# First group of a four-group adapter/FFN kernel: table product behind the fourth mixing step, and the first weight tile made alone among the steps

## The chip, the cores and the metric

One Trainium2 chip, one core of it. The metric is device time in microseconds (us) of one execution, median over runs. TensorE is called PE here, VectorE DVE, ScalarE ACT, GpSimd POOL and SyncE SP; each takes its instructions in the order in which they are written, and they meet only through semaphores.

## The reference, cut to what matters

`x` is 32 x 64 x 1024 in float32, that is 2048 tokens of 1024 columns.

```python
def _L0_cond_ref(x, weights, condition):
    return jnp.einsum('bct,bcd->bdt', x, weights[condition])   # 64 x 64 mix of the rows of a batch
def _L0_ffn_ref(x, W_base, b_base, enc0, enc1, coefs0, coefs1, mask0, mask1):
    base = jnp.einsum('bsd,od->bso', x, W_base) + b_base
    e0, e1 = (jnp.einsum('bsd,rd->bsr', x, e) for e in (enc0, enc1))
    w0, w1 = coefs0 * mask0, coefs1 * mask1
    decoded = jnp.einsum('bsr,eor->ebso', e0, w0) + jnp.einsum('bsr,eor->ebso', e1, w1)
    return base + real_fourier_orthogonal_multiply(decoded).sum(axis=0) * 0.5
# then x = x + L0 ; x = x + sign-weight layer(LoRA gate/up/down MLP(x))
```

The Fourier step is linear. So the first layer is one 1024 x 1024 product with an **effective weight**: W_base plus (encoder rows)^T times a low-rank matrix of 40 rows, and that matrix is the masked, summed coefficients times a fixed 1024 x 1024 Fourier table.

## The kernel before, in words

The tokens go through in four groups of 512 (`g` = 0 to 3). A float32 product is made of three passes over words of a shorter type: high x high, high x low, low x high. ACT writes the high word (`copy`), DVE the low word, the difference (`lo`, L862). Three PE lines, L1404 to L1406, are those three passes.

Each group begins with eight **mixing steps** (`mixing`, `e` = 0 to 7; two for each 128 tokens), which mix the tokens and turn them at once. ACT copies each step's result out twice, DVE makes its low word. Then comes the **first layer**, eight products `first_layer(u)`, each with one weight tile of 128 output columns; `u` = 0 and 1 are cut in two halves of 256 tokens, of which half 0 needs only the first four mixing steps.

In the first group the effective weight must be made first. Its parts:

- SP loads, in this order: x tiles 0 to 2, coefficients and masks, x tile 3, encoder rows, the table (2 MB in four loads), W_base tiles 0 to 3, the bias columns, W_base tiles 4 to 7. There are four slots for W_base tiles: the load of tile u from 4 on waits until tile u-4 is turned (`base_turned`, `load_base`, L277).
- `adapter_sum` (DVE) makes the sums of the coefficients; `low_rank_product` (PE, L1648) multiplies them by the table, into PSUM banks 6 and 7.
- `low_rank_rows` (DVE, L1286 to L1290, then `stacked`, L1265 and L1269) forms the low-rank matrix as the sum and the difference of the two banks, with its words. 120 stacked rows hold the three passes, so a weight tile is one pass.
- `turn_base(u)` (DVE, L1252) transposes a W_base tile, `weight_pair(v)` (PE, L1637) makes the low-rank part of two tiles in banks 2 to 5, `add_weight(u)` (DVE, L1260) adds it, `made_unit(u)` (ACT, then DVE) splits the tile into words, `store_weight(u)` (a DMA on ACT's queue) puts it to memory for the groups to come.

PE's order in the first group: steps 0 to 5, table product, steps 6 and 7, pair 0, first layer 0 and 1 with pair 1 between, pair 2, first layer 2 and 3, pair 3, first layer 4 to 7, then the ranks of the next layer (L1477). DVE's order behind the steps is `effective_weight` and then `first_layer_all`: for each u the total of tile u (`x1_total`, L1033), for some u an `add_weight`, a transpose of a later weight ("beside"), `made_unit(3 + u)`, the low word of the total and the low words of the beside weight. The semaphore `w_added` counts added tiles.

POOL issues the loads of the adapters: A factors first (16 loads), then B factors (16), then 32 small ones.

Of the kernel before, what the change touches and what calls it, by code (L numbers as in the profile page):

```python
# [29 lines left out]
P = 128  # L30
H = 1024
# [68 lines left out]
WEIGHT_BANKS = 2  # L100
# [15 lines left out]
def build_layers(nc, x, cond_index, lora_index, cond_w, W_base, b_base, enc0, enc1, coefs, masks, fourier, scratch,  # L116
# [6 lines left out]
    with ExitStack() as ctx:  # L123
# [83 lines left out]
        kept_step, wsum_done, g_psum, g_read = sem("kept_step"), sem("wsum_done"), sem("g_psum"), sem("g_read")  # L207
# [55 lines left out]
        def _(sp):  # L263
# [147 lines left out]
            for i in range(2):  # L411
                sp.dma_start(coef[i], coefs[i].rearrange("e (p c) r -> p e (c r)", c=KC)).then_inc(coef_in, 16)
                sp.dma_start(coef_mask[i], masks[i].rearrange("e (p c) r -> p e (c r)", c=KC)).then_inc(coef_in, 16)
            load_x(0, 3)
# [3 lines left out]
            table_rows = fourier.rearrange("(p c) n -> p c n", c=KC)  # L418
            for i in range(4):
                sp.dma_start(table[:, 2 * i:2 * i + 2], table_rows[:, 2 * i:2 * i + 2]).then_inc(table_in[i], 16)  # L420
# [28 lines left out]
        def _(pool):  # L449
# [63 lines left out]
            def group(g):  # L513
                index = chosen(lora_index, g)
                wait(piece_lo, START + LOW_PIECES * g)
# [3 lines left out]
                load_b(index, 0)  # L519
# [61 lines left out]
        def _(act):  # L581
# [182 lines left out]

            def mixing_all(g, weights):
# [15 lines left out]
            def first_layer_all(g, making):  # L781

                act.wait_ge(out_psum, START + 8 * g)
                for u in range(KC):
# [6 lines left out]
                    if making and u in (0, 1, 3, 4):  # L791
                        store_weight(u + 4 - u // 3)
# [54 lines left out]
            mixing_ahead(0)  # L847
            mixing_all(0, False)
            for u in range(3):
                made_unit(u)  # L850
                store_weight(u)
            store_weight(3)
# [6 lines left out]
        def _(dve):  # L859
# [359 lines left out]
            def mixing_all(g, weights, beside=None):  # L1219
                for e in range(8):  # L1220
                    if beside is not None:
                        beside(e)
# [32 lines left out]
            def add_weight(u):  # L1255
                dve.wait_ge(base_turned, u + 1)
                dve.wait_ge(w_psum, u // 2 + 1)
                tile = base_t[:, u].rearrange("p (k o) -> p k o", k=KC)
                made = ps[:, WEIGHT_BANKS:WEIGHT_BANKS + 4, :].rearrange("p a (k n o) -> p (a k) n o", k=2, n=2)
                dve.tensor_tensor(tile, made[:, :, u % 2, :], tile, ALU.add).then_inc(w_added, 1)  # L1260

            def stacked(dst, src, column, done):

                low = own_sb[0:STACK, GB + column:GB + column + 1]
                dve.tensor_copy(dst, src).then_inc(g_read, 1)  # L1265
                dve.wait_ge(g_read, done)
                parts = [(dst[:, q], src[:, q]) for q in range(4)] if len(dst.shape) == 4 else [(dst, src)]
                for to, full in parts:
                    last = dve.scalar_tensor_tensor(out=to, in0=to.bitcast(F32), scalar=low, in1=full, op0=ALU.mult,  # L1269
                                                    op1=ALU.add)  # L1270
                last.then_inc(g_read, 1)

            def low_rank_rows(e):

                if e == 1:
                    adapter_sum()
                if e == 3:
                    dve.wait_ge(enc_in, 96)
                    stacked(enc_s.rearrange("r k (q d) -> r q k d", q=4),
                            enc.rearrange("r (q k d) -> r q k d", q=4, k=KC), 0, 1)  # L1280
                if e != 6:
                    return
                turn_base(0)
                near, far = low_rank[:, 0:H // 2], low_rank[:, H // 2:H]
                dve.wait_ge(g_psum, 1)
# [8 lines left out]
            def effective_weight():  # L1294
# [12 lines left out]
                for u in range(5, KC):  # L1307
                    turn_base(u)
# [459 lines left out]
```

## Time and profile before

| | us |
|---|---|
| median of 3 runs | 1940.35 (1940.18 to 1941.18) |
| the profiled execution | 1939.93 |
| its span, first to last instruction | 1938.2 |
| PE busy in the span | 1912.8 (99%) |
| DVE busy | 1493.0 (77%) |
| ACT busy | 763.3 (39%) |
| DMA, mean rate | 113 GB/s |

The profiled execution lies 0.42 us under the median; 1.7 us of it lie outside the span. The page has the busy shares of the engines, a picture of the span in 40 slices, the DMA queues, the chain of work that ended last and the costliest groups of instructions. The first of the 40 slices (the first 48 us) is the only one but for the last with PE below nine tenths. For a stretch this short the order of time is read: the timeline of an engine, with the idle time before an instruction and who ended it.

### The profile page before, as it was taken

The page shows a single profiled execution, that of the slowest core. Times are in us where ns is not written, and L with a number is a line of the kernel's source. Part 1 is how long each engine was busy: PE and PEld are TensorE (multiplying, and loading weights), DVE is VectorE, ACT ScalarE, POOL GpSimd, SP SyncE. Part 2 cuts the span into 40 slices and gives each one's busy share as a digit, 9 for nine tenths or more (in the row PEclk, how much of TensorE's full clock was granted, in tenths as well). Part 3 has the DMA queues.
Part 4 walks back from the last instruction along what each step waited for, and adds up shares of the span by engine and source line. Part 5 has one row for each costly group of instructions (what it writes and reads, how often), then busy time and mean ns, then how long its engine had stood idle before and what let it go on. Part 6 is the DMA issues. An engine that isn't in the chain of part 4 may idle for free.

```text
span 1938.2 us, 31467 instructions
## 1 busy us (share of the span) xinstructions
PE 1912.8 (99%) x9088; PEld 1605.7 (83%) x9088; DVE 1493.0 (77%) x2484; ACT 763.3 (39%) x1450; POOL 543.9 (28%) x935
## 2 busy tenths in 40 slices
PE   6999999999999999999999999999999999999998
PEld 5888888888988888888898888888889888888887
DVE  6977777778778777777777877777877787777786
ACT  3453333334344343333344434333335443334331
POOL 6442222213415212211523322212071322222100
PEclk9999999999999999999999999999999999999999
DMA  9675445543476554444447655454334655555411
GB/s 245 152 147 108 103 98 116 121 94 82 126 149 127 106 115 100 101 99 88 119 116 143 124 113 110 106 116 99 70 102 131 139 121 110 121 110 113 99 44 44
DMA packets 320629, 219.43 MB, mean 113 GB/s; under 512 B 177192, under 2 KB 311208, under 8 KB 320544
## 3 DMA queue, kind: packets, MB, share of 16 engines
q1 hardware_dynamic: 281952, 189.47, 43.5%
q0 software_dynamic: 36352, 24.19, 7.0%
q10 hardware_dynamic: 2240, 4.72, 0.7%
q8 instruction: 42, 0.69, 0.2%
q14 instruction: 43, 0.35, 0.1%
HBM read 205.40 MB, written 12.58 MB: 112 GB/s over the span
## 4 chain that ended last, share of the span: by engine, by line
PE 92%; DVE 4%; issue 2%; ACT 2%; DMA 0%; POOLq 0%; DVEq 0%; ACTq 0%; POOL 0%
PE ps L1404 26%; PE ps L1406 26%; PE ps L1405 26%; PE ps L1611 6%; PE ps L1538 2%; PE ps L1458 2%; PE ps L1459 2%; DVE ps L876 2%; PE ps L1430 1%; PE ps L1477 1%; PE ps L1428 1%; DVE split L862 1%; ACT split L608 0%; ACT hidden L608 0%; PE ps L1648 0%
## 5 line engine op out<-in xcount | busy, mean ns | idle before, releaser
L1404 PE MATMUL ps<-x,split 128*128 128x512 f32 x1376 | 537.7, 391 | 1.3 <-DVE split L862 1.3
L1406 PE MATMUL ps<-x,split 128*128 128x512 f32 x1376 | 536.3, 390 | 0.0
L1405 PE MATMUL ps<-x,split 128*128 128x512 f32 x1376 | 535.4, 389 | 0.0
L608 ACT ACTIVATE split<-ps 128x512 fp32r<-128x512 f32 x344 | 203.0, 599 | 450.8 <-DVE ps L876 438.8
L505 POOL DMA_DIRECT2D nat_ad<-L_cond_A_down x224 | 137.3, 620 | 733.4 <-DVE ps L876 724.3
L1406 PEld LDWEIGHTS ps<-x,split 128*128 128x128 f32 x1376 | 258.3, 188 | 55.8
L1405 PEld LDWEIGHTS ps<-x,split 128*128 128x128 f32 x1376 | 258.4, 188 | 54.8
L1404 PEld LDWEIGHTS ps<-x,split 128*128 128x128 f32 x1376 | 259.0, 188 | 50.0 <-DVE split L862 2.5
L1404 PE MATMUL ps<-hidden 128*128 128x512 f32 x672 | 261.5, 389 | 0.0
L1405 PE MATMUL ps<-hidden 128*128 128x512 f32 x672 | 261.5, 389 | 0.0
L1406 PE MATMUL ps<-hidden 128*128 128x512 f32 x672 | 261.4, 389 | 0.0
L862 DVE TENSOR_TENSOR split<-ps,split 128x512 fp32r<-128x512 f32 (+1 forms) x376 | 243.4, 685 | 19.3 <-ACT split L608 6.7
L876 DVE STREAM_TRANSPOSE ps<-nat 128x512 f32<-128x512 f32 x344 | 225.5, 701 | 0.5
L1118 DVE TENSOR_TENSOR acc<-ps,acc 128x512 f32<-128x512 f32 x200 | 135.2, 689 | 47.4 <-PE ps L1406 47.4
L499 POOL DMA_DIRECT2D nat_b<-L_cond_B_gate x224 | 124.5, 556 | 161.1 <-DVE ps L876 149.1
L608 ACT ACTIVATE hidden<-ps 128x512 fp32r<-128x512 f32 x184 | 109.2, 599 | 143.3 <-DVE ps L876 136.9
L1404 PEld LDWEIGHTS ps<-hidden 128*128 128x128 f32 x672 | 126.2, 188 | 26.1
L1406 PEld LDWEIGHTS ps<-hidden 128*128 128x128 f32 x672 | 126.2, 188 | 26.1
L1405 PEld LDWEIGHTS ps<-hidden 128*128 128x128 f32 x672 | 126.2, 188 | 25.9
L876 DVE STREAM_TRANSPOSE ps<-nat_down 128x512 f32<-128x512 f32 x176 | 141.0, 846 | 0.0
L1102 DVE TENSOR_TENSOR act_f<-ps,gated 128x512 f32<-128x512 f32 x84 | 58.0, 690 | 97.3 <-PE ps L1459 96.8
L583 ACT ACTIVATE hidden<-act_f 128x512 fp32r<-128x512 f32 (+1 forms) x88 | 55.6, 632 | 188.9 <-DVE act_f L1102 179.9
(137 smaller groups left out, 2830.5 us busy)
## 6 DMA issues: line engine op xcount, KB each, us to landing
nat<-L_cond_W_gate SPq DMA_DIRECT2D x336, 128.0 KB
nat<-L_cond_W_up SPq DMA_DIRECT2D x336, 128.0 KB
nat_down<-L_cond_W_down SPq DMA_DIRECT2D x112, 384.0 KB, 6.4
nat_a<-L_ffn_weight SPq DMA_DIRECT2D x128, 128.0 KB, 2.8
nat<-effective_weight SPq DMA_DIRECT2D x24, 512.0 KB
nat<-x SPq DMA_DIRECT2D x16, 512.0 KB
nat_b<-L_cond_B_gate POOLq DMA_DIRECT2D x224, 24.0 KB, 2.2
nat_b<-L_cond_B_up POOLq DMA_DIRECT2D x224, 24.0 KB, 2.1
```

The costliest lines, as they stand in the source:

```text
L499: pool.dma_start(nat_b[32 * (b // 2):32 * (b // 2) + 32, t, :, b % 2, :], b_rows[t][bass.ds(part, 1), bass.ds(i, 1)].rearrange("q a f b c ...
L505: pool.dma_start(nat_ad[b % 2::2, b // 2, :], ad_rows[bass.ds(part, 1), bass.ds(i, 1)].rearrange("q a f r c -> (q a f) r c"))\
L583: return act.activation(dst, src, ACT.Copy)
L608: act.activation(dst, src, func).then_inc(piece_hi, 1)
L862: return dve.tensor_tensor(dst, full, hi.bitcast(F32), ALU.subtract)
L876: dve.transpose(dst, src).then_inc(piece_turned, 1)
L1102: dve.tensor_tensor(act_f[:], ps[:, (2 * j + 1) % 3, :], gated[:], ALU.mult).then_inc(up_read, 1)
L1118: dve.tensor_tensor(acc[:, i, :], ps[:, DOWN_BANKS[i], :], acc[:, i, :], ALU.add).then_inc(down_added, 1)
L1404: pe.matmul(dst, a[0], b[0], start=first, stop=False)
L1405: pe.matmul(dst, a[0], b[1], start=False, stop=False)
L1406: return pe.matmul(dst, a[1], b[0], start=False, stop=last)
L1611: mm = pe.matmul(ps[:, OUT_BANKS[o], :], signs[:, m, P * o:P * o + P], down(s, m), start=(m == 0 and s == 0), stop=(m == KC - 1 and s == 1))
```

## The change

All of it is in the first group (`g` = 0).

- **SP**: the four table loads are issued ahead of x tile 3 and the encoder rows.
- **POOL**: the B factors are loaded first; the A factors wait until the table product is done.
- **PE**: the table product stands behind step 3 instead of step 5. The eight weight tiles are made in five products instead of four: tile 0 alone, behind step 5, in banks 6 and 7; tiles 1 and 2 between the halves of first layer 0; 3 and 4 between the halves of first layer 1; 5 and 6 ahead of first layer 3; 7 ahead of first layer 5. Each but the first two waits until all tiles of the one before it are added.
- **DVE and ACT**: the banks of the table product are copied out by both engines. The words of the low-rank matrix are made for tiles 0 to 2 first and for the others later. Tiles 0 and 1 are added, split and awaited by halves of their rows. The first copy of the encoder rows moves from DVE to ACT. The orders of both engines are written out (`mixing_first`). DVE now adds tiles 3 to 7 in first-layer steps u = 0 to 4 (before: tiles 4 to 7 in steps 0, 1, 3, 4).

```diff
+MADE = ((0,), (1, 2), (3, 4), (5, 6), (7,))
+MADE_BANKS = (6, 2, 2, 2, 4)
+LOW_COLUMNS = (slice(0, 96), slice(96, 256))
...
+            for i in range(4):
+                sp.dma_start(table[:, 2 * i:2 * i + 2], table_rows[:, 2 * i:2 * i + 2]).then_inc(table_in[i], 16)
             load_x(0, 3)
...
-            for i in range(4):
-                sp.dma_start(table[:, 2 * i:2 * i + 2], table_rows[:, 2 * i:2 * i + 2]).then_inc(table_in[i], 16)
             for u in range(BASE_SLOTS):
                 load_base(u)
...
+                if g == 0:
+                    load_b(index, 0)
+                    wait(g_psum, 1)
                 wait(piece_lo, START + LOW_PIECES * g)
                 load_a(index, A_gate, 0)
                 wait(piece_turned, PIECES * g)
                 load_a(index, A_up, 1)
-                load_b(index, 0)
+                if g > 0:
+                    load_b(index, 0)
...
+            def made_halves(u):
+                slot_read(0, 0, SPLIT_W + u)
+                hi = split[:, (SPLIT_W + u) % SPLIT_SLOTS, 0, :]
+                act.wait_ge(half_added, u + 1)
+                copy(hi[:, 0:512], base_t[:, u, 0:512]).then_inc(half_hi, 1)
+                act.wait_ge(w_added, u + 1)
+                copy(hi[:, 512:], base_t[:, u, 512:]).then_inc(plain_hi, 1)
...
@@ ScalarE, mixing_first @@
+                mixing(0, 2)
+                act.wait_ge(enc_in, 96)
+                copy(enc_s.rearrange("r k (q d) -> r q k d", q=4),
+                     enc.rearrange("r (q k d) -> r q k d", q=4, k=KC)).then_inc(enc_step, 1)
+                mixing(0, 3)
+                cond(0, 3)
+                act.wait_ge(enc_step, 2)
+                act.wait_ge(g_psum, 1)
+                copy(enc[:, 0:512], ps[0:STACK, 6, :]).then_inc(g_moved, 1)
+                for e in range(4, 6):
+                    mixing(0, e)
+                made_halves(0)
+                for e in range(6, 8):
+                    mixing(0, e)
+                store_weight(0)
+                made_halves(1)
+                store_weight(1)
+                made_unit(2)
+                store_weight(2)
...
@@ VectorE @@
+            def low_rank_words(i):
+                cols = LOW_COLUMNS[i]
+                even, odd = (enc[:, 512 * h:512 * h + 512].rearrange("r (q c) -> r q c", q=2)[:, :, cols] for h in range(2))
+                whole, words = (t.rearrange("r (q c) -> r q c", q=4) for t in (low_rank, low_s))
+                dve.wait_ge(g_moved, 2)
+                dve.tensor_tensor(whole[:, 0:2, cols], even, odd, ALU.add)
+                dve.tensor_tensor(whole[:, 2:4, cols], even, odd, ALU.subtract).then_inc(low_step, 1)
+                dve.wait_ge(low_step, 3 * i + 1)
+                dve.tensor_copy(words[:, :, cols], whole[:, :, cols]).then_inc(low_step, 1)
+                dve.wait_ge(low_step, 3 * i + 2)
+                dve.scalar_tensor_tensor(out=words[:, :, cols], in0=words[:, :, cols].bitcast(F32),
+                                         scalar=own_sb[0:STACK, GB + 1:GB + 2], in1=whole[:, :, cols], op0=ALU.mult,
+                                         op1=ALU.add).then_inc(low_step, 1)
...
@@ VectorE, mixing_first @@
+                mixing(0, 3)
+                cond(0, 3)
                 turn_base(0)
+                low_rank_out()
+                low_rank_words(0)
+                for e in range(4, 6):
+                    mixing(0, e)
+                add_weight(0)
+                made_low_half(0, 0)
+                mixing(0, 6)
+                made_low_half(0, 1)
+                mixing(0, 7)
                 turn_base(1)
+                low_rank_words(1)
+                add_weight(1)
                 turn_base(2)
+                for half in range(2):
+                    made_low_half(1, half)
+                add_weight(2)
                 turn_base(3)
                 made_unit(2)
+                for u in range(4, KC):
                     turn_base(u)
...
                     x1_total(g, u)
-                    if making and u in (0, 1, 3, 4):
-                        add_weight(u + 4 - u // 3)
+                    if making and u < 5:
+                        add_weight(3 + u)
...
@@ TensorE @@
+                    if by_halves and half == 0 and k == 0:
+                        pe.wait_ge(half_lo, u + 1)
+                    if by_halves and half == 0 and k == 4:
+                        pe.wait_ge(plain_lo, 4 + u + 1)
...
+            def make_weights(v):
+                tiles = MADE[v]
                 if v == 0:
+                    pe.wait_ge(low_step, 3)
+                elif v == 1:
                     pe.wait_ge(mixed_lo, 8)
                     pe.wait_ge(xt_copied, 8)
                 else:
+                    pe.wait_ge(low_step, 6)
+                    pe.wait_ge(w_added, MADE[v - 1][-1] + 1)
...
                 if making:
                     first_layer(g, 0, 0)
+                    make_weights(1)
                 first_layer(g, 0, 1)
                 for u in range(1, KC):
-                    if making and u in (1, 2, 4):
-                        weight_pair((u + 2) // 2)
+                    if making and u in (3, 5):
+                        make_weights((u + 3) // 2)
                     if u == 1:
                         if making:
                             first_layer(g, 1, 0)
+                            make_weights(2)
                         first_layer(g, 1, 1)
```

## Rows read from the trace of the kernel before

**Rows 1.** The page: busy us of each engine, share of the span, instructions.
```profile
PE 1912.8 (99%) x9088; PEld 1605.7 (83%) x9088; DVE 1493.0 (77%) x2484; ACT 763.3 (39%) x1450; POOL 543.9 (28%) x935
```

**Rows 2.** Stretches: length; busy PE, PEld, DVE, ACT, POOL; granted clock; DMA share, GB/s.
```profile
30.00:40.00 10.00, 4.81 (x34) 3.97 (x32) 8.75 (x10) 3.21 (x5) 7.70 (x14) 0.88 1.16 170
...
80.00:90.00 10.00, 10.00 (x46) 8.25 (x45) 10.00 (x16) 5.47 (x10) 5.39 (x7) 1.00 0.87 177
```

**Rows 3.** Timeline of PE: start, length, instruction; in brackets idle before, releaser.
```profile
20.59 0.36 PE L1428 MATMUL ps<-mix,split 128*128 128x256 f32 x1 [0.32 <-DVE mix L862]
...
23.78 7.03 PE L1648 MATMUL ps<-fourier_table,wsum 128*120 128x512 f32 x16
...
36.34 1.20 PE L1637 MATMUL ps<-low_s,enc_s 120*128 120x256 f32 x8 [2.73 <-DVE turned L862]
...
41.34 0.58 PE L1404 MATMUL ps<-turned,split 128*128 128x256 f32 x1 [3.80 <-DVE split L862]
...
56.22 0.39 PE L1404 MATMUL ps<-turned,split 128*128 128x512 f32 x1
...
61.70 0.39 PE L1404 MATMUL ps<-turned,split 128*128 128x512 f32 x1
...
67.14 1.12 PE L1637 MATMUL ps<-low_s,enc_s 120*128 120x256 f32 x8
...
68.39 0.47 PE L1404 MATMUL ps<-turned,split 128*128 128x512 f32 x1
...
90.44 4.00 PE L1477 MATMUL ps<-x,hidden 128*128 128x256 f32 x32
```

**Rows 4.** Stretches around PE's two long waits, columns as in rows 2.
```profile
37.50:38.00 0.50, 0.03 (x1) 0.00 (x0) 0.35 (x1) 0.00 (x0) 0.50 (x2) 0.63 1.03 106
...
41.30:44.40 3.10, 3.06 (x14) 3.07 (x15) 3.07 (x3) 1.06 (x1) 2.99 (x6) 0.50 1.05 321
44.40:48.50 4.10, 4.10 (x36) 4.10 (x35) 0.42 (x1) 0.00 (x0) 3.71 (x8) 0.99 1.13 297
```

**Rows 5.** Timeline of DVE.
```profile
25.25 1.28 DVE L862 TENSOR_TENSOR turned<-ps,turned 128x512 fp32r<-128x512 f32 x2
...
30.85 0.69 DVE L1286 COPY low_rank<-ps 120x512 f32<-120x512 f32 x1 [3.17 <-PE ps L1648]
...
33.75 1.28 DVE L1269 SCALAR_TENSOR_TENSOR low_s<-low_s,own_sb,low_rank 120x1024 fp32r<-120x1024 f32 x1
...
49.78 1.22 DVE L1260 TENSOR_TENSOR base_t<-ps,base_t 128x1024 f32<-128x1024 f32 x1 [4.96 <-PE ps L1637]
...
54.47 3.49 DVE L1252 STREAM_TRANSPOSE base_t<-base 128x1024 f32<-128x1024 f32 x3
57.88 0.71 DVE L1033 SCALAR_TENSOR_TENSOR acc<-ps,b_col,acc 128x512 f32<-128x512 f32 x1
...
63.33 1.22 DVE L1260 TENSOR_TENSOR base_t<-ps,base_t 128x1024 f32<-128x1024 f32 x1
```

**Rows 6.** Timeline of ACT.
```profile
60.19 1.56 ACT L583 ACTIVATE lora_b<-ps 64x256 fp32r<-64x256 f32 x4 [0.93 <-DVE ps L876]
...
73.39 1.06 ACT L583 ACTIVATE split<-base_t 128x1024 fp32r<-128x1024 f32 x1 [2.90 <-DVE base_t L1260]
```

**Rows 7.** Issues on SP's queue in three stretches, each with its times to landing.
```profile
L420 SPq DMA_DIRECT2D fourier_table<-fourier x4: 352/432/432, 10.6 to 11.9; - x4
...
DMA to landing us min/median/max: 6.4/7.7/10.2
...
L277 SPq DMA_DIRECT2D base<-L_ffn_W_base x3: 431/433/451, 36.6 to 37.5; - x3
DMA to landing us min/median/max: 3.7/3.9/3.9
...
L277 SPq DMA_DIRECT2D base<-L_ffn_W_base x4: 437/471/1050, 43.6 to 45.7; - x4
DMA to landing us min/median/max: 6.0/6.4/7.2
```

More of the change, by code:

```diff
@@ L846, in _ @@
             act.activation(gated[:, 0:1], lora_b_rem[:, 0, 0, 0:1].bitcast(F32), ACT.Silu)
[L847 to L852, printed above, removed]
+            mixing_first()
             first_layer_all(0, True)
@@ L1217, in made_unit, with made_low_half, mixing_all @@
                 lo(split[:, s, 1, :], base_t[:, u], split[:, s, 0, :]).then_inc(plain_lo, 1)
-            def mixing_all(g, weights, beside=None):
+            def made_low_half(u, half):
+                s = (SPLIT_W + u) % SPLIT_SLOTS
+                cols = slice(512 * half, 512 * half + 512)
+                if half == 0:
+                    dve.wait_ge(half_hi, u + 1)
+                else:
+                    dve.wait_ge(plain_hi, 4 + u + 1)
+                lo(split[:, s, 1, cols], base_t[:, u, cols], split[:, s, 0, cols]).then_inc((half_lo, plain_lo)[half], 1)
+            def mixing_all(g, weights):
                 for e in range(8):
-                    if beside is not None:
-                        beside(e)
                     mixing(g, e)
@@ L1255, in add_weight @@
             def add_weight(u):
+                v, n = MADE_OF[u]
                 dve.wait_ge(base_turned, u + 1)
-                dve.wait_ge(w_psum, u // 2 + 1)
+                dve.wait_ge(w_psum, v + 1)
                 tile = base_t[:, u].rearrange("p (k o) -> p k o", k=KC)
[L1259 to L1271, printed above, removed]
@@ L1294, in effective_weight @@
-            def effective_weight():
+                tiles = len(MADE[v])
+                made = ps[:, MADE_BANKS[v]:MADE_BANKS[v] + 2 * tiles, :]\
+                    .rearrange("p a (k n o) -> p (a k) n o", k=4 // tiles, n=tiles)[:, :, n, :]
+                if u < 2:
+                    dve.tensor_tensor(tile[:, 0:4], made[:, 0:4], tile[:, 0:4], ALU.add).then_inc(half_added, 1)
+                    dve.tensor_tensor(tile[:, 4:], made[:, 4:], tile[:, 4:], ALU.add).then_inc(w_added, 1)
+                else:
+                    dve.tensor_tensor(tile, made, tile, ALU.add).then_inc(w_added, 1)
@@ new lines, in enc_words @@
+            def enc_words():
+                low = own_sb[0:STACK, GB:GB + 1]
+                dst = enc_s.rearrange("r k (q d) -> r q k d", q=4)
+                src = enc.rearrange("r (q k d) -> r q k d", q=4, k=KC)
+                dve.wait_ge(enc_step, 1)
+                for q in range(4):
+                    last = dve.scalar_tensor_tensor(out=dst[:, q], in0=dst[:, q].bitcast(F32), scalar=low, in1=src[:, q],
+                                                    op0=ALU.mult, op1=ALU.add)
+                last.then_inc(enc_step, 1)
@@ L1307, in effective_weight @@
-                for u in range(5, KC):
+                for u in range(4, KC):
                     turn_base(u)
@@ L1435, in first_layer @@
                 m = SPLIT_W + u
-                pe.wait_ge(plain_lo, 12 * g + 4 + u + 1)
+                by_halves = g == 0 and u < 2
+                if not by_halves:
+                    pe.wait_ge(plain_lo, 12 * g + 4 + u + 1)
                 if half == 0:
```

76 lines of the change are left out of this document (35 added, 41 removed).

## The prediction

> **What bounds the kernel now.** I read the shares first: PE is busy 99% of the span, no other engine over 77% [rows 1]. So a change of the first group can only win back PE's idle time, and the stretches say where that is: in 30 to 40 us PE is busy for 4.81 us, and in 80 to 90 us it is full again, but so is DVE [rows 2]. PE's timeline names the waits: 2.73 us ahead of pair 0 and 3.80 us ahead of first layer 0, both ended by DVE [rows 3]. The granted clock then stands at 0.50 (1.2 GHz) from 37.6 us until PE has worked again from 41.34 to 44.4 us [rows 4]; those 3.1 us of work cost about 1.5 us. Together some 8 us, 0.4% of the time, can be won.
>
> The second thing to see is DVE. It waits 4.96 us for pair 1 and from 49.78 us on has one instruction behind the other [rows 5]. At 57.88 it takes the total of tile 0, without a wait for PE, so PE is ahead of it there. PE goes without a break from 41.34 to the ranks at 90.44 [rows 3], but with a full DVE beside it. Whatever makes PE earlier than DVE's list must be paid back as a wait.
>
> **The change, part by part.** All times below are on the clock of the profiled execution (1939.93 us, span 1938.2), which is 0.42 us under the median of the runs; the sum is made against it and then moved by 0.42.
>
> *Table product.* Steps 4 and 5 begin at 20.59 and the product at 23.78 [rows 3]; put ahead of them it begins near 20.1, as soon as step 3 is through, and ends 7.03 us later, at 27.1 instead of 30.8. It needs the table, which landed between 17.0 and 22.1 when issued at 10.6 to 11.9 [rows 7]. Issued ahead of x tile 3, whose issue waits, it lands some 5 us sooner, in time. x tile 3 and the encoder rows come behind its 2 MB. Only ACT's copies hang on them; ACT takes them in order, so a late tile delays the copies of steps 2 and 3, which nothing needs before PE takes up step 4 at 27. Cost nothing; cover 4 us and more.
>
> *POOL.* The B factors come sooner, the A factors some 10 us later, behind the wait for the table product; behind that wait stand the 32 small loads and nothing else that is urgent: the A factors are turned in first-layer step 3, 40 us later. Cost nothing on this list.
>
> *DVE's chain from 27.1 us.* A 1024-wide DVE instruction takes 1.22 us alone and 1.15 in a row (3.49 for three), a 512-wide one 0.69 and 0.60 (1.28 for two) [rows 5]. Copy out 0.7; words for tiles 0 to 2 (two adds of 192 columns, a cast and a scaled add of 384, by width from these rows and 1.28 for 1024) 1.7: 29.5. Low words of steps 4 and 5, each behind two ACT copies of 0.6: 31.6. Tile 0 by halves 1.3, its ACT half copy 0.7, low half 0.6: 34.2, where first layer 0 can start. Step 6's low word waits about 1 us for ACT, whose half copies stand ahead of it; with the second half and step 7: 36.5. Turn tile 1, other words (2.2), add tile 1, turn 2, two low halves, add 2, turn 3: 45.7. Some 15 handovers between engines add 0.4: 46.1. Low word of tile 2, turns 4 to 7: 51.9, if the tiles are there.
>
> *W_base tiles 4 to 7.* This is a wait that before hardly shows. SP issues tile 7 only when tile 3 is turned, now at 46.1, in four loads 0.44 us apart, so the last at 47.5. Times to landing: 3.7 to 3.9 us where little was queued, 6.0 to 7.2 us behind three other tiles [rows 7]. So tile 7 lands between 51.2 and 54.7; with only tile 6 ahead of it I take the near end, 51.4. DVE then begins tile 7 at 51.4 instead of 50.8 and the total of tile 0 at 52.5, against 57.88 before.
>
> The Trainium skill says (DMA: Bandwidth & Descriptors, Issuing engines are not separate DMA queues) that loads issued by SP, ACT and POOL run on the same 16 engines and interleave. It speaks against POOL's part: the A factors now travel beside W_base tiles 5 and 6, which by that rule would move the landing towards the far end. No row separates the two; the range holds both ends.
>
> *First-layer steps 0 and 1 on DVE.* Before, from the total of tile 0 to the end of the add in step 1 took 63.33 + 1.22 - 57.88 = 6.67 us [rows 5]. Now the tile split in a step is the one added in it, so DVE waits for ACT's 1.06 us copy, which starts behind the add [rows 6], with only a short transpose between: 0.9 us a step, and 0.3 us more behind the 1.56 us of ACT copies [rows 6]. Step 0 has these waits in full: 7.85 us. So the fifth tile (tile 4) is added at 52.5 + 7.85 = 60.4.
>
> *PE.* First layer 0 starts at 34.2 instead of 41.34. It waits 0.7 us for its second half, then 1.5 us for tile 1, and reaches the end of first layer 2 at about 56, where before that was 61.70 [rows 3]. There the third product of two tiles (5 and 6) waits for five added tiles: until 60.4, a **new wait of 4.4 us**. Before, the same kind of wait stood one first layer later and cost nothing. Then: this product 0.96 us, five first layers of 5.5 us (56.22 to 61.70 is 5.48; 68.39 to 90.44 is four of 5.51), tile 7's product 0.6 (half of 0.96; up to 0.96 if its cost is by instruction): 29.1. The ranks begin at 89.5, against 90.44: **0.9 us won**.
>
> *The clock.* The wait before lasted 4.0 us, with 1.2 us of pair 0 inside, when the clock fell [rows 3, 4]. A wait of 4.4 us without work is more idle than that, so I take the fall, and the cost that the same fall had before: 1.5 us, now on PE's path, since from there PE has no slack. Bounds: 0 (no fall) to 2.5 us. The Trainium skill has it so (TensorE: Matmul & The Clock Gate, What's actually happening): the lower level is the default to which an idle TensorE falls back. By that rule the sum is 0.6 us slower, without it 0.9 us faster.
>
> Sum: -0.9 + 1.5 = +0.6 us, 1940.5 in the profiled execution, **1941.0** as a median. The five first layers, and all 1840 us behind the ranks, stay as they are.
>
> **The rivals.** *A: the wait at tiles 5 and 6 doesn't come.* Then PE keeps its lead of 5.7 us: 1934.6. For it: PE's idle before is as large. Against it: DVE's instructions from 27.1 to the fifth add sum up to 29 us even with no wait among them, so 56.1 at the earliest, and its waits for ACT and loads are real. A gain over 0.2% needs the fifth add by 57.4. Chance 0.08.
>
> *B: the W_base tiles come late.* If tile 7 lands 7.2 us after its last issue or worse (54.7), the fifth add is at 63.8, PE's wait is 7.7 us, and the time is 4.0 us longer: 1944.4, growing one for one. It decides from a landing at 54.6 on. For it: stores of the finished weight tiles (512 KB each) and POOL's loads fall into the same stretch. Against it: SP's queue ahead of tile 7 is shorter than before. Chance 0.14.
>
> *C: the clock stays.* The wait is cut by an early tile 7 or the fall comes too late to matter: 1939.4. Chance 0.2.
>
> *D: the table product isn't earlier.* If the table lands late after all, at 22.1 as before, the chain begins 2 us later: 1943. The issue time speaks against it. Chance 0.03.
>
> My forecast has 0.55.
>
> **How the numbers follow.** A measurement of this kernel tells 0.2% (3.9 us) from no change. Faster by more: A, and a little of C: 0.09. Slower by more: B: 0.14. Within: 0.77. For the range, low: no wait for tile 7, DVE's chain 0.6 us shorter, no fall, 2.5 us faster, rounded down to 1937.5. High: B with little over its bound, 1944.5. A and the tail of B are left out.
>
> **What would show it.** Right: in the trace of after the table product starts near 20.1; the first product of the first layer near 34; DVE's total of tile 0 between 51.5 and 55; PE idle 3 to 8 us ahead of the product for tiles 5 and 6, ended by an add of DVE, with the clock at 0.50 behind it; from there no wait to the ranks. Wrong: a wait there under 2 us (A), a DVE wait of over 3 us ahead of the last turned tile (B), the clock at 1.00 through the wait (C), or any change of duration behind 95 us.

## The result, and the profile after

The changed kernel takes 1943.53 us (median; 1942.18 to 1944.5), the kernel before, on the same chips, 1940.29 (1939.25 to 1941.58). The ratio is 1.0015, with a 95% interval from 1.0009 to 1.0021: 3.2 us or 0.17% slower, under the 0.2% that the prediction took as the bound, though the interval ends just above it. The predicted median was 1941.0, with a range of 1937.5 to 1944.5; the time lies in the range, near its upper end. Of all executions below one, with the products later, took 4995 us; it is left out.

| | before | after |
|---|---|---|
| the profiled execution | 1939.93 | 1943.57 |
| its span | 1938.2 | 1941.9 |
| PE busy | 1912.8 | 1913.9 |
| the table product starts | 23.78 | 20.48 |
| first layer 0 starts | 41.34 | 34.45 |
| the ranks start | 90.44 | 94.13 |

The last row says where to look: the ranks come 3.69 us later, the whole span is 3.7 us longer, so nothing behind them has changed. The page's line of busy times stands for [rows 1]:

```profile
PE 1913.9 (99%) x9096; PEld 1606.2 (83%) x9096; DVE 1493.8 (77%) x2491; ACT 764.7 (39%) x1454; POOL 543.1 (28%) x935
```

Next the stretches of [rows 2], with the same columns (length; busy PE, PEld, DVE, ACT, POOL; granted clock; DMA share, GB/s):

```profile
30.00:40.00 10.00, 9.34 (x77) 8.97 (x76) 8.21 (x14) 4.33 (x9) 7.77 (x14) 1.00 1.10 202
80.00:90.00 10.00, 10.00 (x46) 8.28 (x45) 9.47 (x15) 4.65 (x8) 5.28 (x6) 1.00 0.84 193
```

From 30 to 40 us PE is now busy for 9.34 us instead of 4.81. That gap is closed. PE's timeline (start, length, instruction; in brackets the idle time before and who ended it) shows what came of it, in the places of [rows 3]:

```profile
20.48 7.13 PE L1733 MATMUL ps<-fourier_table,wsum 128*120 128x512 f32 x16
...
30.24 1.05 PE L1722 MATMUL ps<-low_s,enc_s 120*128 120x128 f32 x8
...
34.45 0.36 PE L1476 MATMUL ps<-turned,split 128*128 128x256 f32 x1 [0.31 <-DVE split L904]
...
43.45 0.35 PE L1476 MATMUL ps<-turned,split 128*128 128x256 f32 x1 [1.45 <-DVE split L904]
...
62.54 2.04 PE L1722 MATMUL ps<-low_s,enc_s 120*128 120x256 f32 x8 [6.68 <-DVE base_t L1316]
64.38 0.63 PE L1476 MATMUL ps<-turned,split 128*128 128x512 f32 x1
...
76.89 1.01 PE L1722 MATMUL ps<-low_s,enc_s 120*128 120x128 f32 x8
77.73 0.44 PE L1476 MATMUL ps<-turned,split 128*128 128x512 f32 x1
...
94.13 0.40 PE L1555 MATMUL ps<-x,hidden 128*128 128x256 f32 x2
```

The waits of 2.73 and 3.80 us are gone, and first layer 0 starts 6.9 us earlier. At the end of first layer 2 it is still 5.8 us ahead (55.86 instead of 61.70). All of that and more is given back in one place: PE stands 6.68 us ahead of the product of tiles 5 and 6, until DVE (L1316) has added the low-rank part of the fifth tile. DVE's timeline, in the places of [rows 5], says why that add ends only at 62.39 (a "turn" is DVE's transpose of a W_base tile):

```profile
44.96 1.23 DVE L1301 STREAM_TRANSPOSE base_t<-base 128x1024 f32<-128x1024 f32 x1
46.23 1.23 DVE L904 TENSOR_TENSOR split<-base_t,split 128x1024 fp32r<-128x1024 f32 x1
47.37 3.49 DVE L1301 STREAM_TRANSPOSE base_t<-base 128x1024 f32<-128x1024 f32 x3
53.45 1.25 DVE L1301 STREAM_TRANSPOSE base_t<-base 128x1024 f32<-128x1024 f32 x1 [2.59 <-DMA base<-L_ffn_W_base]
54.62 0.71 DVE L1075 SCALAR_TENSOR_TENSOR acc<-ps,b_col,acc 128x512 f32<-128x512 f32 x1
...
61.18 1.21 DVE L1316 TENSOR_TENSOR base_t<-ps,base_t 128x1024 f32<-128x1024 f32 x1
```

The first row is the turn of tile 3; its end, 46.19, frees the slot for W_base tile 7. The fourth is the turn of tile 7, which waits 2.59 us for that load. So the total of tile 0 (L1075) is at 54.62 and the fifth add 7.77 us later. The loads of tile 7 themselves, as in [rows 7] (SP's issues, then the times to landing, that is, until the data are there):

```profile
L285 SPq DMA_DIRECT2D base<-L_ffn_W_base x4: 312/696/1572, 46.2 to 49.1; - x4
...
  DVE base_t L1301: 2.6, 1
...
DMA to landing us min/median/max: 4.3/4.9/5.1
```

Last the stretches around the wait, as in [rows 4]:

```profile
50.00:55.80 5.80, 5.80 (x28) 4.55 (x26) 3.21 (x4) 0.00 (x0) 4.40 (x9) 1.00 0.38 66
55.90:62.50 6.60, 0.00 (x0) 0.00 (x0) 5.59 (x9) 2.99 (x7) 5.01 (x9) 0.88 0.29 86
62.50:67.70 5.20, 5.16 (x16) 4.51 (x17) 4.07 (x7) 3.08 (x6) 0.00 (x0) 0.50 0.26 102
67.70:76.00 8.30, 8.30 (x38) 6.78 (x38) 7.18 (x11) 4.50 (x8) 0.00 (x0) 1.00 0.43 153
```

After 55.9 us PE does nothing; the mean clock of 0.88 there means that it fell near the end of the wait. The work from 62.54 on runs at 0.50 (1.2 GHz) until 67.7: 0.63 us for a product that takes 0.39 at 1.00.

### The profile page after: what moved, and what is told of

It is laid out like the page before. It is cut to its first block, busy times and chain, and to the rows that moved or that the text cites. A ratio compares the mean times of both kernels' runs of the same rounds, so it can differ in the third digit from the quotient of the medians.

```text
span 1941.9 us, 31500 instructions
## 1 busy us (share of the span) xinstructions
PE 1913.9 (99%) x9096; PEld 1606.2 (83%) x9096; DVE 1493.8 (77%) x2491; ACT 764.7 (39%) x1454; POOL 543.1 (28%) x935
## 4 chain that ended last, share of the span: by engine, by line
PE 91%; DVE 4%; ACT 2%; issue 2%; DMA 1%; POOLq 0%; SPq 0%; DVEq 0%; ACTq 0%; POOL 0%
PE ps L1476 25%; PE ps L1478 25%; PE ps L1477 25%; PE ps L1689 6%; PE ps L1616 2%; PE ps L1536 2%; PE ps L1537 2%; DVE ps L918 2%; PE ps L1502 1%; PE ps L1555 1%; PE ps L1500 1%; DVE split L904 1%; ACT split L620 0%; ACT hidden L620 0%; PE ps L1733 0%
## 5 line engine op out<-in xcount | busy, mean ns | idle before, releaser
L1478 PEld LDWEIGHTS ps<-x,split 128*128 128x128 f32 x1376 | 258.3, 188 | 55.9
```

Of the source, the lines that this page charges most:

```text
L1478: return pe.matmul(dst, a[1], b[0], start=False, stop=last)
```

## The experiments

The runs set one theory against its rivals. Theory 1 is that of the prediction: PE's lead ends at the product of tiles 5 and 6, which waits for DVE's list; the list is held up by W_base tile 7, and the clock falls in the wait. The rivals: the other moves of the change (the table ahead of x tile 3, POOL's order) cost something by themselves, or the first group is bound elsewhere, so that taking this wait away moves it and wins nothing. Each expectation below names its own rival, as theory 2 or by a letter.

Time medians are compared with the kernel before as it ran beside them. Single executions of these kernels begin the table product anywhere from 19.9 to 21.7 us, with no edit that would explain it. So, where traces are compared, the time from the start of the table product to the ranks is used as well: 73.65 us in the profile of after, 70.9 in the prediction.

### The clock alone: the wait filled with unused products

```diff
+                    if making and u == 3:
+                        for k in range(27):
+                            pe.matmul(ps[:, 1, :], split[:, (SPLIT_W + 2) % SPLIT_SLOTS, 0, 0:P], mixed[:, 0, 0],
+                                      start=True, stop=True)
```

> Against the changed kernel, 27 products whose result is not used (some 6.1 us of work, into a bank that first layer 3 overwrites) stand in PE's wait ahead of the product of tiles 5 and 6; nothing else is changed, and DVE's list is untouched. Theory 1 (2.5 us of the loss are the lower clock that the wait brings): the clock stays at 1.00, the product of tiles 5 and 6 starts within 0.3 us of 62.5, the ranks 2.2 to 2.5 us sooner: 1941.1 us. Rival (the clock costs nothing, DVE is the bound behind it): 1943.5 us.

Measured: 1940.80 us, before 1940.96, ratio 1.0001 (0.9992 to 1.001). PE's timeline and one stretch of this kernel:

```profile
56.44 6.28 PE L1745 MATMUL ps<-turned,split 128*128 128x512 f32 x27
62.83 1.20 PE L1722 MATMUL ps<-low_s,enc_s 120*128 120x256 f32 x8
...
92.25 0.52 PE L1555 MATMUL ps<-x,hidden 128*128 128x256 f32 x3
```

```profile
40.00:92.00 52.00, 50.44 (x265) 42.95 (x264) 46.53 (x63) 20.15 (x35) 24.36 (x39) 1.00 0.64 160
```

The product of tiles 5 and 6 starts no earlier (62.83 against 62.54), but the clock stays at 1.00, and from the end of the fifth add (62.69) to the ranks it takes 29.56 us instead of 31.74. So the fall of the clock costs **2.2 us** of the changed kernel, on PE's path, as the prediction had it, and without it the change is worth nothing either way. By the changed kernel's own rows it is nearer 2.5: the product of tiles 5 and 6 takes 1.84 us to the next instruction instead of 0.96, and the eight products behind it start 0.43 us apart instead of 0.23. In the run with the wait filled, both weight products take 0.08 us more and that of tile 7 starts 0.16 us late, so its 29.56 is not quite free of waits. The medians of the two kernels lie further apart, 3.4 us against their kernels before; 0.5 us of that is a fifth add that came earlier in this trace (41.39 us behind the start of the table product instead of 41.91), and the rest is within the intervals.

That difference can be read in each run in which the same work follows the same add. The second column is what of the stretch at 0.50 lies in work, the third the time from the fifth add to the ranks, less 29.56:

| | PE's wait | work at 0.50 | price |
|---|---|---|---|
| after | 6.68 | 5.2 | 2.2 |
| small loads behind tile 7 | 4.86 | 5.4 | 2.2 |
| store of tile 2 later | 5.80 | 3.4 | 1.3 |
| both | 4.42 | 5.8 | 2.4 |
| POOL's order as before | 5.98 | 4.4 | 1.8 |
| table behind, as before | 6.42 | 3.6 | 1.4 |
| turn of tile 7 later | 3.10 | 3.4 | 1.3 |

The price is about 0.4 us for each us of work at 0.50 (up to 0.5, if 29.56 is 0.3 too long), and it does not go with the length of the wait: the longest of these waits costs less than the second shortest.

### The load of W_base tile 7: what stands beside it

Three edits, one on POOL's queue, one on ACT's, and both at once:

```diff
+                if g == 0:
+                    wait(base_turned, KC)
                 load_rest(index)
```

> The changed kernel with POOL's 32 small loads behind the transpose of W_base tile 7. Theory A (the small loads slow SP's issue and the landing of tile 7): its four loads are issued within 1.8 us of the transpose of tile 3, the last lands 5.3 us or less after that transpose ends (changed kernel: 2.9 us and 7.2 us), and DVE's wait for tile 7 is under 1 us. Theories B (the store of tile 2) and C (the way from the transpose to the landing is as long with nothing beside it): 7 us, a wait of 2.4 to 2.7 us.

```diff
-                store_weight(2)
...
+                    if making and u == 0:
+                        store_weight(2)
                     if making and u < 5:
                         store_weight(3 + u)
```

> The changed kernel with the store of weight tile 2 (512 KB) moved from 45.2 us into first-layer step 0, some 10 us later. Theory B (that store slows the landing of tile 7): the last of tile 7's loads lands 5.7 us or less after the transpose of tile 3 ends (changed kernel: 7.2 us), DVE's wait for it 1.2 us or less. Theories A and C: 7 us, a wait of 2.4 to 2.7 us.

> Both edits at once: POOL's small loads wait for the last turned tile, and the store of weight tile 2 is issued in first-layer step 0. Nothing of the first group's weights but tile 7 is then in flight from 47 us on. Theory 1 (the landing is set by what shares the DMA engines, and the two add up): tile 7 lands 4.5 to 5.0 us behind the end of the turn of tile 3 (7.2 in the profile of after, 5.4 and 6.4 with one edit alone), DVE's wait ahead of the last turn is under 0.6 us, the fifth add ends 14.2 to 14.6 us behind the end of the turn of tile 3, where the prediction had 14.3, and PE's wait ahead of the product of tiles 5 and 6 is 4.0 to 4.8 us; the clock falls all the same. Theory 2 (one cause, seen twice): the landing stays at 5.4 us or later, the wait of DVE at 0.8 us.

Measured, one execution each: 1942.87, 1941.84 and 1942.87 us. The timeline of DVE has, in each, the turn of tile 3 and that of tile 7, first with the small loads later, then with the store later, then with both:

```profile
45.99 1.23 DVE L1303 STREAM_TRANSPOSE base_t<-base 128x1024 f32<-128x1024 f32 x1
...
52.67 1.25 DVE L1303 STREAM_TRANSPOSE base_t<-base 128x1024 f32<-128x1024 f32 x1 [0.78 <-DMA base<-L_ffn_W_base]
```

```profile
44.98 1.23 DVE L1302 STREAM_TRANSPOSE base_t<-base 128x1024 f32<-128x1024 f32 x1
...
52.60 1.25 DVE L1302 STREAM_TRANSPOSE base_t<-base 128x1024 f32<-128x1024 f32 x1 [1.37 <-DMA base<-L_ffn_W_base]
```

```profile
46.11 1.24 DVE L1304 STREAM_TRANSPOSE base_t<-base 128x1024 f32<-128x1024 f32 x1
...
52.35 1.25 DVE L1304 STREAM_TRANSPOSE base_t<-base 128x1024 f32<-128x1024 f32 x1 [0.33 <-DMA base<-L_ffn_W_base]
```

From the end of the first to the start of the second it is 7.26 us in the profile of after, 5.45 with the small loads later, 6.39 with the store later, 5.00 with both. In the other runs, in which neither was touched, tile 7 landed 6.5 to 7.4 us behind the turn of tile 3. So POOL's small loads are the larger part. The store is the smaller: its 6.39 is hardly outside the spread, and lies between what that run's expectation had for a guilty store (5.7 or less) and for an innocent one (7). With both out of the way the fifth add ends 13.95 us behind the turn of tile 3 (16.20 in after, 14.3 in the prediction's sum), PE's wait is 4.42 us (4.4 predicted), and the clock falls all the same:

```profile
61.45:67.20 5.75, 5.75 (x18) 4.88 (x19) 4.63 (x7) 3.04 (x6) 5.41 (x11) 0.50 0.35 101
```

From the table product to the ranks it is 71.56 us instead of 73.65. That the time of this one execution did not follow is its late start: its table product began at 21.73, 1.25 us behind that of after.

The DMA queues from 45 to 54 us (packets, MB, share of the 16 engines' time), in after: q1 has SP's loads, q10 ACT's store, q0 POOL's small loads.

```profile
q1 hardware_dynamic: 1136, 1.03, 53.2%
q10 hardware_dynamic: 170, 0.60, 18.1%
q0 software_dynamic: 549, 0.08, 8.7%
```

And with the small loads later:

```profile
q1 hardware_dynamic: 1152, 1.05, 44.1%
q10 hardware_dynamic: 195, 0.68, 20.5%
```

0.08 MB of small loads took half the time of a store of 0.60 MB, and SP's loads of about the same size took 53.2% instead of 44.1% beside them. That the packets stand in each other's way within an engine fits this; it is inferred from the shares, no row shows it directly. The shares do not rank the landings either: with the store later SP's loads took 60.9%, more than in after, and tile 7 landed sooner.

### POOL's order as before

```diff
-                if g == 0:
-                    load_b(index, 0)
-                    wait(g_psum, 1)
...
-                if g > 0:
-                    load_b(index, 0)
+                load_b(index, 0)
```

> The order of POOL's loads as in the kernel before (A factors first, without a wait for the table product); all else as changed. Theory 1: what makes W_base tile 7 land late is whatever POOL has in flight beside it at 46 to 53 us. With the small loads no longer held back behind the A factors they are issued earlier or later by where the A factors stand; if they still stand beside tile 7, it lands 6.6 to 7.3 us behind the end of the turn of tile 3, as in the runs whose loads are unaltered, and the time is 1943 to 1944; if they are out of the way, some 5.4 us behind it, as in the run with the small loads behind tile 7, PE's wait ahead of the product of tiles 5 and 6 is 4.9 us and the time about 1.5 us less. Theory 2 (POOL's order is without effect, as the prediction priced it): landing and time are those of the changed kernel within 0.5 us.

Measured: 1943.45 us in one execution. Tile 7's turn starts 6.57 us behind that of tile 3, at the near edge of what theory 1 named, with the small loads still beside it; PE waits 5.98 us. It tells little: the order of the A and B factors is not the cause, since the A factors are through POOL's issue by 40.5 us and the small loads begin at about 41 us either way, so that about half of the 32 stand beside tile 7 in both.

### The table behind x tile 3 and the encoder rows, as before

```diff
-            table_rows = fourier.rearrange("(p c) n -> p c n", c=KC)
-            for i in range(4):
-                sp.dma_start(table[:, 2 * i:2 * i + 2], table_rows[:, 2 * i:2 * i + 2]).then_inc(table_in[i], 16)
             load_x(0, 3)
...
+            table_rows = fourier.rearrange("(p c) n -> p c n", c=KC)
+            for i in range(4):
+                sp.dma_start(table[:, 2 * i:2 * i + 2], table_rows[:, 2 * i:2 * i + 2]).then_inc(table_in[i], 16)
```

> The changed kernel with SP's order of before: the table behind x tile 3 and the encoder rows; PE's order stays as changed. In the four traces with the table ahead PE starts at 12.7 to 13.4 us, before at 12.2 us. Theory 2 (the table's 2 MB travel beside the small loads of the mixing matrices, which come 0.5 to 1.2 us later, and everything behind them too): PE starts near 12.2 us, the table product still begins right behind step 3, for its last quarter is needed only 5 us after its start; everything 0.5 to 1 us sooner: 1942.5 to 1943 us on the scale on which the changed kernel is 1943.5. Rival (the table is then late, as the prediction's rival D has it): the product stops for the last quarter, up to 2 us: 1944 to 1945.5 us.

Measured: 1943.19 us, before 1940.99, ratio 1.0013 (1.0004 to 1.0022), not told apart from the changed kernel. PE's timeline has

```profile
21.09 7.03 PE L1733 MATMUL ps<-fourier_table,wsum 128*120 128x512 f32 x16
```

with no wait, though the last of the table's four loads landed only at 23.0, 1.9 us into the product, which takes them in order. The time lies between what the two theories named (1942.5 to 1943 and 1944 to 1945.5). So this part of the change was not needed for the earlier product.

### The products of tiles 5 to 7 one first layer later

```diff
-                    if making and u in (3, 5):
-                        make_weights((u + 3) // 2)
+                    if making and u in (4, 6):
+                        make_weights(u // 2 + 1)
```

> Against the changed kernel (1943.5 us), only the products of tiles 5 and 6 and of tile 7 stand one first layer later on PE (ahead of first layers 4 and 6). Theory 1 (the loss is PE's wait for the fifth added tile, paid for a second time by the clock): the 6.7 us wait shrinks to about 3 us, now ended by the low words of tile 3 near 58.9 us; some 1 to 2 us come back as waits for totals ahead of first layers 4 and 5; ranks 1.2 us sooner with the clock down, 3.7 us sooner with the clock up: 1940 to 1942.3 us. Rival (the place of the products doesn't matter, DVE's list alone sets the end): ranks where they were, 1943.5 us.

Measured: 1942.05 us, before 1940.96, ratio 1.0006 (0.9997 to 1.0015), some 2 us better than the changed kernel. The trace is of another execution, of 1941.67 us:

> The same kernel as e1_products_later, for a profile at the usual clock. Theory 1: PE's wait ahead of first layer 3 is about 3 us and ended by the low words of tile 3 on DVE; further waits of 1 to 2 us ahead of first layers 4 and 5, ended by totals on DVE; ranks at 90.5 to 93 us.

```profile
58.42 0.50 PE L1476 MATMUL ps<-turned,split 128*128 128x512 f32 x1 [3.08 <-DVE split L904]
...
66.94 0.47 PE L1476 MATMUL ps<-turned,split 128*128 128x512 f32 x1 [1.83 <-DVE acc L1075]
...
91.35 0.28 PE L1555 MATMUL ps<-x,hidden 128*128 128x256 f32 x1
```

Its stretches around the two waits:

```profile
58.40:65.10 6.70, 6.68 (x32) 5.53 (x32) 5.49 (x8) 3.73 (x8) 4.31 (x8) 1.00 0.29 86
65.10:67.30 2.20, 0.37 (x3) 0.34 (x3) 2.10 (x4) 0.02 (x1) 0.00 (x0) 1.00 0.00 0
67.30:70.70 3.40, 3.40 (x10) 2.63 (x9) 2.59 (x4) 2.63 (x5) 0.00 (x0) 0.50 0.38 154
```

The wait of 6.68 us is gone, but 3.08 us stand one product later (first layer 3 needs the words of tile 3, which hang on the same late DVE) and 1.83 one later still (first layer 4, until DVE has taken the total of an earlier tile). The clock stood at 1.00 from 58.4 to 67.3, behind the first of these waits, and at 0.50 for 3.4 us behind the second. DVE's lateness goes on to the next that needs it: the rival that the bound only moves is true for 4.9 of the 6.7 us.

### The turn of tile 7 one step later

```diff
-                for u in range(4, KC):
+                for u in range(4, 7):
                     turn_base(u)
...
+                    if making and u == 0:
+                        turn_base(7)
                     beside_turn(g, u)
```

> Against the changed kernel, only DVE's transpose of W_base tile 7, which waited 2.6 us for its load, stands behind the add of tile 3 in first-layer step 0. Theory 1 (DVE's wait for tile 7's landing lies on PE's path): the total of tile 0 comes 3.7 us sooner, the fifth add 3.4 us sooner (59.0 us), PE's wait is 3.1 us; 1940.1 us if the clock falls all the same, 1937.6 us if it stays at 1.00. Rival (the transpose waits as long in its new place, and DVE is late again by as much): 1943 us or more.

Measured: 1939.62 us, before 1940.96, ratio 0.9995 (0.9986 to 1.0004). DVE's timeline, then the stretches:

```profile
47.82 3.49 DVE L1301 STREAM_TRANSPOSE base_t<-base 128x1024 f32<-128x1024 f32 x3
51.23 0.71 DVE L1075 SCALAR_TENSOR_TENSOR acc<-ps,b_col,acc 128x512 f32<-128x512 f32 x1
...
53.64 1.25 DVE L1301 STREAM_TRANSPOSE base_t<-base 128x1024 f32<-128x1024 f32 x1 [0.18 <-DMA base<-L_ffn_W_base]
...
58.06 1.21 DVE L1316 TENSOR_TENSOR base_t<-ps,base_t 128x1024 f32<-128x1024 f32 x1
```

```profile
56.40:59.40 3.00, 0.00 (x0) 0.01 (x1) 2.95 (x6) 0.04 (x1) 2.96 (x6) 1.00 0.09 6
59.43:62.80 3.37, 3.37 (x12) 3.08 (x13) 2.29 (x4) 3.02 (x6) 1.52 (x3) 0.50 0.47 164
```

Nobody needs tile 7 before first layer 7. Its turn, put behind the fourth add, hides the load: DVE idles 0.18 us for it instead of 2.59, and the turn itself fills the time in which DVE had waited for ACT's copy. The fifth add ends at 59.27, PE's wait is 3.10 us, and the time is some 4.6 us under that of the changed kernel (1.34 under before here, 3.24 over it there).

### Both moves

The products one first layer later, and the turns of tiles 6 and 7 in first-layer steps 0 and 1:

```diff
-                for u in range(4, KC):
+                for u in range(4, 6):
                     turn_base(u)
...
+                    if making and u < 2:
+                        turn_base(6 + u)
                     beside_turn(g, u)
```

> Both edits, with the transpose of tile 6 moved into step 0 and that of tile 7 into step 1. Theory 1: PE waits under 1 us ahead of first layers 3 to 5, the clock stays at 1.00, the ranks begin at 85.5 to 87 us instead of 94.1 (before: 90.4): 1935 to 1936.5 us, faster than both kernels. Rival (DVE's list as a whole is the bound, its waits only move): ranks near 90 us, 1939.5 to 1941 us.

Measured: **1936.91 us**, before 1940.96, ratio 0.9981 (0.9972 to 0.999). PE's timeline from 40 to 92 us has, behind a first wait of 1.46 at 43.85, only these:

```profile
61.55 1.12 PE L1724 MATMUL ps<-low_s,enc_s 120*128 120x256 f32 x8
62.91 0.47 PE L1478 MATMUL ps<-turned,split 128*128 128x512 f32 x1 [0.25 <-DVE acc L1075]
...
69.07 0.47 PE L1478 MATMUL ps<-turned,split 128*128 128x512 f32 x1 [0.46 <-DVE acc L1075]
...
86.40 3.51 PE L1557 MATMUL ps<-x,hidden 128*128 128x256 f32 x28
90.54 0.39 PE L1557 MATMUL ps<-x,hidden 128*128 128x256 f32 x1 [0.63 <-DVE x L904]
```

```profile
40.00:92.00 52.00, 49.20 (x272) 42.51 (x272) 47.90 (x66) 21.89 (x41) 25.80 (x40) 1.00 0.72 174
```

Here the lead that the change gives PE is kept: 65.51 us from the table product to the ranks instead of 73.65, which is the wait (6.68) and the clock (2.2), less waits of 0.25 and 0.46 us that come in. The clock stays at 1.00. What is left is DVE, busy for 47.9 of these 52 us.

The same with the table loads behind x tile 3 and the encoder rows again:

> Two parts at once: the products of tiles 5, 6 and 7 one first layer later with the turns of tiles 6 and 7 in the first-layer steps (the version that gave 1936.9), and the table loads again behind x tile 3 and the encoder rows, as in the kernel before. Theory 1 (moving the table ahead gives nothing, since it lands in time either way): 1936.9 within 0.8 us, ratio to before 0.9975 to 0.9985, ranks at 86 to 87 us. Theory 2 (the table lies in wait for the product as soon as PE has no slack left): the table product is interrupted or starts 0.5 to 2 us later, and with no wait left on PE's path this shows in full: 1937.5 to 1939.

Measured: **1935.90 us**, before 1941.06, ratio 0.9975 (0.9965 to 0.9984), the fastest version, and 1.0 us under the time of its twin, where theory 1 allowed 0.8. From the table product (20.04) to the ranks (85.48) it takes 65.44 us, as with the table ahead. Theory 2 (the table is late when PE has no slack) is wrong. It lies 1.1 us further under the kernel before than its twin, and the pair above lay 1.0 apart in the same sense; in neither pair do the intervals part. In the traces PE's first step starts between 12.4 and 13.4 us in the nine traces with the table ahead, between 11.9 and 12.8 in the four with it behind. That step waits for the mixing matrices, which POOL loads: ACT's first copy of them starts between 11.6 and 12.6 us with the table ahead, between 11.1 and 12.0 with it behind. That the table's 2 MB, then in flight beside them, delay them fits that; the two ranges overlap, and it is not shown.

### The kernel before once more

> The kernel before once more, nothing altered. It tells whether PE's first mixing step at 12.20 us, from which the prediction's times count, is usual. If the change moves it (12.96 us in the profile of after), this run has 12.2 again; if it varies from execution to execution, it lies anywhere between 12.2 and 13.1, and the time from the first step to the ranks (78.2 us in the profile of before) is the number to compare.

Measured: 1940.88 us in one execution. PE starts at 12.07 (12.20 in [rows 3]'s trace) and reaches the ranks at 91.33: 79.3 us instead of 78.2. The two waits are the same, 2.73 and 3.80, but the clock stood at 0.50 from 35.3 to 45.6 us, instead of 37.6 to 44.4, and pair 0 took 2.05 us instead of 1.20. So the profile on which the prediction rests was an execution with a short stretch at 0.50: here 5.6 us of work lay in it instead of 3.1, and the ranks came 1.0 us later from the first step, again 0.4 us for each us.

## Why the prediction came out as it did

The ranks were predicted at 91.0 and came at 94.13: 3.1 us late in the trace. The median missed by less, 2.5 us, because the prediction raised its sum by 0.42 us for a profile of before that lay under its median, while that of after lies at its median. By the prediction's own steps:

1. **Table product**: start 20.1 and end 27.1 predicted, 20.48 and 27.61 measured. Right within half a microsecond. That the table had to come ahead for it was an unneeded part of the change, priced rightly at nothing on this path; a price of up to 1 us at the start of the program stays open.
2. **DVE's chain**: the turn of tile 3 was to end at 46.1 and ended at 46.19; first layer 0 was to start at 34.2 and started at 34.45; the wait for tile 1 was 1.45 (1.5), and first layer 2 ended at 55.86 (about 56). Right, built by width and count from rows of the kernel before, with some luck in the end: the chain began 0.5 us late, with the table product, and ran 0.4 us shorter than the 19.0 us of its sum.
3. **W_base tile 7**: this term was mis-sized. Predicted 5.3 us behind the turn of tile 3 (51.4), measured 7.26 (53.45): **+2.0 us**. The choice between the rows' ends (51.2 to 54.7) was made on SP's queue, "with only tile 6 ahead of it I take the near end". What decided was not SP's queue but what other engines had in flight: with POOL's small loads and one store out of the way the landing came 5.0 us behind the turn. The prediction had a sentence of the Trainium skill beside it that pointed this way (DMA: Bandwidth & Descriptors, Issuing engines are not separate DMA queues: loads issued by different engines share the 16 DMA engines and interleave); the runs agree, 5.0 against 7.3 us, except that the loads at fault are the small ones, which the prediction charged with nothing, not the A factors. The argument against rival B, a shorter queue on SP, was the wrong reading. Of the two parts of this term, the issues ended at 49.1 instead of 47.5, and the last landed 4.3 us behind instead of 3.9; but with the store later they ended 1.3 us after the turn, as predicted, and the tile still landed 6.4 us after it.
4. **First-layer steps 0 and 1 on DVE**: 7.85 predicted from the total of tile 0 to the fifth add, 7.77 measured. Right, the wait of 0.83 for ACT's copy included.
5. **PE's new wait**: 4.4 predicted, 6.68 measured; the difference is step 3. The place, the waiting product and the releaser are those predicted.
6. **The clock**: the fall came; the price was mis-sized, 2.2 us against 1.5 (**+0.7**; 2.5, or +1.0, by the rows of after). The 1.5 was taken from the one stretch of [rows 4] with 3.1 us of work at 0.50. The work at 0.50 was 5.2 us here, and in other executions 3.4 to 5.8, and the price goes with it. The bounds, 0 to 2.5 us, hold all of these. The rule of the Trainium skill cited there (TensorE: Matmul & The Clock Gate, What's actually happening: an idle TensorE falls back to the lower level) agrees with the wait of 6.68 us. Which shorter waits bring the fall the runs leave open: behind 3.10 us, in the run with the turn of tile 7 later, the work ran at 0.50, behind 3.08 us, in the run with the products later, at 1.00.
7. **From the add to the ranks without a fall**: 29.1 predicted, 29.56 measured in the run with the wait filled (**+0.46**; +0.2 by the rows of after, with the price of 2.5). Tile 7's product is 0.24 of it: 128 columns instead of 256 were taken to cost 0.6, and cost 0.84 in after from its start to the next product.

1.99 + 0.68 + 0.46 is the whole miss of 3.1 us. The sign was forecast for the right reason: PE's gain of 6.9 us at first layer 0 is paid back as a wait behind DVE, and the clock's price comes on top. But its size was not: the loss is 3.2 us where 0.6 was forecast, all three errors point the same way, and the time is in the range only because its upper end was drawn from rival B. The forecast sign hung on 1.5 us for the clock against 0.9 us won; by the late tile alone, with no fall of the clock, the change comes out even (1940.8). Rival B was half true: tile 7 came late, but by 2 us, short of the landing at 54.6 from which B decided. Rival A is what the last two edits make of the change, and they give 1936.9 and 1935.9, where A had 1934.6. Rival C is the run with the wait filled, 1940.8; C's 1939.4 was lower, for it did not have the late tile.

What the change as it stands lacks is in the code: it asks DVE to turn tiles 6 and 7 before the first total, though first layers 6 and 7 need them some 30 us later, and it asks PE for tiles 5 and 6 at first layer 3, though first layer 5 needs them first.

## What to carry to other kernels

When a change gives one engine a head start, list for the next engine in line what it still has to do in order, loads included, and find the first consumer that now meets it; the head start ends there, and work that nobody needs soon is to be moved behind that point in the list. The landing time of a load on the critical list is not read from its own queue: look at what every other queue has in flight in those microseconds, small transfers above all. A wait of PE of some microseconds can cost more than itself, by what of the work behind it runs at the lower clock.

## What the runs showed of the hardware

- Small loads weighed far more than their bytes: 0.08 MB of them took 8.7% of the DMA engines' time from 45 to 54 us, a store of 0.60 MB 18.1%, and without them a load of four times 128 KB landed 1.8 us sooner.
- How SP's four issues of tile 7 are spaced did not set the landing: they took 1.3 us (46.2 to 47.5) with the store later, 2.9 us (46.2 to 49.1) in after, and the tile landed 6.4 and 7.3 us behind the turn; with both edits they took 2.5 us and it landed after 5.0.
- Eight products of 128 columns, each with other weights, took 1.01 us, and of 256 columns 1.12: half the columns saved a tenth of the time.
- The work at 0.50 behind a wait lasted 3.4 to 5.8 us and cost 0.4 us for each us; it was 3.4 us behind a wait of 3.10 us and 5.8 behind one of 4.42. Between the waits of 3.08 and 1.83 us in the run with the products later no work ran at 0.50; behind the second 3.4 us did.
